# ScalarE evaluates silu of the gate in both routed runs and in ten of the sixteen shared products of a macaron layer

## The chip, the core and the metric

The kernel runs on one core of a Trainium2 chip. The metric is device time in microseconds (us); lower is better. The core's engines are called by their short names: PE (TensorE, matmuls and transposes), ACT (ScalarE), DVE (VectorE), POOL (GpSimd) and SP (SyncE, which only issues DMAs here). Each works through its own instructions in order; semaphores tie them together.

## The reference

The layer is `x + ffn/2`, then `x + ssm`, then `x + ffn/2`, each behind a layernorm, on 4 x 512 tokens of width 256. The feed-forward part stands twice and is what the change touches:

```
logits = x @ router_w                       # 8 experts, top 1
score = sigmoid(max(logits))
xs = x * score
for e in range(8):                          # each token goes to its one expert
    h = silu(xe @ gate_w[e]) * (xe @ up_w[e])
    out = out + where(token of e, h @ down_w[e], 0)
shared = silu(x @ shared_gate_w) * (x @ shared_up_w) @ shared_down_w
return out + shared
```

The part between the two is a state-space scan over 512 time steps with 16 states for each of 256 channels, in four sequences.

## The kernel before

Five semaphored programs, one for each engine, are written out by hand, so the order in the source is the order on each engine. All data is float32. There are two feed-forward runs, `r = 0` (to about 110 us of the trace) and `r = 1` (from about 331 us), and the scan stage stands between them.

**Shared products.** For each run, each of four sequences `b` and each half `fo` of the hidden width, PE computes gate and up into two PSUM banks (L865, `shared_gate_up`), ACT writes `tanh(gate/2)` to `sh_th` (L565, `shared_tanh`), and DVE makes `sh_q = (tanh+1)*gate` (L1181) and then `sh_q*up` (L1184), both in `shared_hidden`. That is 2*silu(gate)*up. PE multiplies it by the shared down weights (L845, `shared_down`), and DVE adds a quarter of the result to `x_sb` (L1286, `shared_result`); the quarter undoes the factor of 2 and applies the half of the layer. The products of `(1, 0)` are made in four smaller pieces within the scan stage (`tanh_piece`, `hidden_piece`).

**Routed runs.** Tokens are gathered by expert into 18 tiles `j` of 128 rows, even ones of one expert (whole), odd ones of four experts with 32 rows each (mixed). For a tile, PE does `gate_up(j)` (L904 for whole, L901 for mixed tiles), then `turn(j)`, which transposes the product of tile `j-1` (L914) and the gathered rows of tile `j+1` (L919), then `down(j-2)` (L941, L938). ACT does `tanh(j)` (L580), with the token's half score as its scale, then `copy(j)` of the transposed block out of PSUM (L585), then copies of expert weights (L593). DVE does `q = (tanh+1)*gate` (L1309), `h = q*up` (L1314), the scaling of the result of tile `j-2` (L1324 in run 0, L1327 in run 1), and copies of expert weights (L1296). POOL gathers rows and scatters results by indirect DMA. `gate_up(j+1)` needs `copy(j)`, and `turn(j+1)` needs `h(j)`.

**Around them.** Behind run 0, `combine` adds the scattered results, `stats_of` and `normalise` make the second layernorm, `ln_transposes` (L793) turns it, and `project` (L969) begins the scan's inputs. Ahead of run 1, `route` and `row_ids` on DVE make the list of tokens, between the shared products. ACT evaluates functions by tables; where one is needed that is not there, the program has an ACT_TABLE_LOAD.

Of the kernel before, what the change touches and what calls it, by code (L numbers as in the profile page):

```python
# [15 lines left out]
ALU = mybir.AluOpType  # L16
ACT = mybir.ActivationFunctionType
# [10 lines left out]
def macaron_kernel(nc, x, w_xT, w_dtT, b_dt, a_log, d_skip, router_w, gate_w, up_w, down_w,  # L28
# [5 lines left out]
    KC = D // P  # L34
# [41 lines left out]
    with ExitStack() as ctx:  # L76
# [3 lines left out]
        def sem(name):  # L80
# [132 lines left out]
        ff_gu, ff_tanh, ff_mul, ff_hidden, ff_tp, ff_tpc, ff_y, ff_yc = (  # L213
            sem(f"ff_{s}") for s in ("gu", "tanh", "mul", "hidden", "tp", "tpc", "y", "yc"))
# [33 lines left out]
        def shared_banks(r, b, fo):  # L248

            return (H[0], H[1]) if fo == 0 else (YS[0], YS[1]) if r == 1 or b in (0, 3) else (T, Y)  # L250

# [297 lines left out]
        def _(act):  # L549
# [10 lines left out]
            def shared_tanh(r, b, fo):  # L560
                u = 2 * BATCH * r + 2 * b + fo
                act.wait_ge(sh_gu, u + 1)
                if u >= 2:
                    act.wait_ge(sh_mul, u - 1)
                nc.scalar.activation(sh_th[:, u % 2], shared_banks(r, b, fo)[0], ACT.Tanh, scale=0.5).then_inc(sh_tanh, 1)  # L565
# [9 lines left out]
            def routed(r):  # L575
                def tanh(j):
                    act.wait_ge(ff_gu, NR * r + j + 1)
                    if r > 0 or j >= 2:
                        act.wait_ge(ff_mul, NR * r + j - 1)
                    nc.scalar.activation(th[:, j % 2], H[j % 2][:, 0:F], ACT.Tanh, scale=xr[:, j % XR, D:D + 1]).then_inc(ff_tanh, 1)  # L580

                def copy(j, lo=0, hi=4):

                    act.wait_ge(ff_tp, (NR + 2) * r + j + 2)
                    nc.scalar.activation(tt[:, (j + 1) % 2, lo:hi], T[:, lo * P:hi * P].rearrange("p (a t) -> p a t", t=P),  # L585
                                         ACT.Copy).then_inc(ff_tpc, 1)

                def part_dn(i, g):

                    e = act.value_load(part_expert(i, g), min_val=0, max_val=E - 1)  # L590
                    if i >= 2:
                        act.wait_ge(ff_y, NR * r + 2 * i - 2)
                    nc.scalar.activation(dn_part(i, g), w_dn[:, :, bass.ds(e, 1), :].squeeze(2), ACT.Copy).then_inc(wc_dn, 1)  # L593

                act.wait_ge(rt_expert, r + 1)
                if r == 0:
                    act.wait_ge(experts_in, 16 * 3 * KC)
                copy(-1, lo=2)
                for j in range(NR):
                    tanh(j)  # L600
                    copy(j, lo=2 if j == 0 else 0, hi=2 if j == NR - 1 else 4)
                    for g in ((1, 2) if j % 2 == 0 else (3,)):
                        part_dn(j // 2, g)
                copy(NR, hi=2)
# [119 lines left out]
            shared_tanh(0, 0, 0)  # L724
            route_copy(0)
            route(0)
            shared_tanh(0, 0, 1)
            for fo in range(KC):
                shared_tanh(0, 1, fo)
            routed(0)  # L730
            act.wait_ge(a_log_in, 16)
            nc.scalar.activation(a_exp[:], a_in[:], ACT.Exp).then_inc(a_ready, 1)
            act.wait_ge(a_ready, 1)
            nc.scalar.activation(a_neg[:], a_exp[:], ACT.Copy, scale=-1.0).then_inc(a_ready, 1)
            for fo in range(KC):
                shared_tanh(0, 2, fo)
            shared_tanh(0, 3, 0)
# [6 lines left out]
            shared_tanh(0, 3, 1)  # L744
# [10 lines left out]
            for fo in range(KC):  # L755
                shared_tanh(1, 1, fo)
            ln_copies(2, BATCH - 1)
            route_copy(1)
            route(1)
            for b in range(2, BATCH):  # L760
                for fo in range(KC):
                    shared_tanh(1, b, fo)
# [389 lines left out]
        def _(dve):  # L1152
# [23 lines left out]
            def shared_hidden(r, b, fo):  # L1176
# [3 lines left out]
                gate, up = shared_banks(r, b, fo)  # L1180
                nc.vector.scalar_tensor_tensor(out=sh_q[:, fo], in0=sh_th[:, fo], scalar=1.0, in1=gate,  # L1181
                                               op0=ALU.add, op1=ALU.mult).then_inc(sh_mul, 1)
                dve.wait_ge(sh_mul, u + 1)
                nc.vector.tensor_tensor(hidden_rows(r, b)[:, fo], sh_q[:, fo], up, ALU.mult).then_inc(sh_hidden, 1)  # L1184

            def hidden_piece(p):
# [5 lines left out]
                dve.wait_ge((half_mul, sh_mul)[h], n)  # L1192
# [3 lines left out]
            def route(r):  # L1196
# [14 lines left out]
                nc.vector.tensor_scalar(xn_no[:, :, D], score[:, 2], 0.5, None, ALU.mult)  # L1211
                nc.vector.scalar_tensor_tensor(out=xn_no[:, :, D + 1], in0=score[:, 2], scalar=0.25, in1=score[:, 2],
                                               op0=ALU.mult, op1=ALU.mult).then_inc(rt_score, 1)
# [91 lines left out]
            def routed(r):  # L1305
                def hidden(j):
                    u = j % 2
                    dve.wait_ge(ff_tanh, NR * r + j + 1)
                    nc.vector.scalar_tensor_tensor(out=q_sb[:, u], in0=th[:, u], scalar=1.0, in1=H[u][:, 0:F],  # L1309
                                                   op0=ALU.add, op1=ALU.mult).then_inc(ff_mul, 1)  # L1310
                    dve.wait_ge(ff_mul, NR * r + j + 1)
                    if j >= 2:
                        dve.wait_ge(ff_tp, (NR + 2) * r + j + 1)
                    nc.vector.tensor_tensor(h_sb[:, u], q_sb[:, u], H[u][:, F:], ALU.mult).then_inc(ff_hidden, 1)  # L1314
# [222 lines left out]
```

## Time and profile before

| | us |
|---|---|
| median of three runs | 443.85 |
| fastest and slowest of them | 442.93, 444.07 |
| span of the profiled execution | 441.9 |
| PE busy | 403.1 (91%) |
| DVE busy | 349.3 (79%) |
| POOL busy | 280.9 (64%) |
| ACT busy | 271.2 (61%) |

No own time is listed for the profiled execution apart from its span, from its first to its last instruction. The median lies 1.95 us above that span. A row of a timeline gives the start, the duration, the engine, the line, the operation, what it writes and reads, how many instructions are merged in it, and in brackets the idle time of the engine before it with what ended that.

### The profile page before, as it was taken

The page shows a single profiled execution, that of the slowest core. Times are in us where ns is not written, and L with a number is a line of the kernel's source. Part 1 is how long each engine was busy: PE and PEld are TensorE (multiplying, and loading weights), DVE is VectorE, ACT ScalarE, POOL GpSimd, SP SyncE. Part 2 cuts the span into 40 slices and gives each one's busy share as a digit, 9 for nine tenths or more (in the row PEclk, how much of TensorE's full clock was granted, in tenths as well). Part 3 has the DMA queues.
Part 4 walks back from the last instruction along what each step waited for, and adds up shares of the span by engine and source line. Part 5 has one row for each costly group of instructions (what it writes and reads, how often), then busy time and mean ns, then how long its engine had stood idle before and what let it go on. Part 6 is the DMA issues. An engine that isn't in the chain of part 4 may idle for free. (4 is left out here: it accounts for less than half of the span.)

```text
span 441.9 us, 8372 instructions
## 1 busy us (share of the span) xinstructions
PE 403.1 (91%) x2716; PEld 278.5 (63%) x2716; DVE 349.3 (79%) x564; ACT 271.2 (61%) x498; POOL 280.9 (64%) x216
## 2 busy tenths in 40 slices
PE   6899899999896899899989998989999898899995
PEld 6437444444354689777977797879984556344442
DVE  5689666674598988999999999989886876567762
ACT  1410555564148799897999899997952110556552
POOL 7204356543337589997999799989881006577543
PEclk9899999999999999999999999999999999999998
DMA  8968115942604227463537353452320634234411
GB/s 257 384 181 251 48 59 174 296 163 85 202 34 66 73 79 177 85 143 108 182 75 132 133 168 74 119 158 94 122 58 0 196 91 117 92 117 135 120 52 44
DMA packets 50808, 56.84 MB, mean 129 GB/s; under 512 B 16329, under 2 KB 35597, under 8 KB 50768
## 3 DMA queue, kind: packets, MB, share of 16 engines
q1 hardware_dynamic: 46624, 45.78, 35.5%
q0 software_dynamic: 4144, 10.54, 8.0%
q8 instruction: 23, 0.38, 0.3%
q14 instruction: 17, 0.14, 0.1%
HBM read 41.14 MB, written 16.48 MB: 130 GB/s over the span
## 5 line engine op out<-in xcount | busy, mean ns | idle before, releaser
L515 POOL TENSOR_TENSOR gs<-hs,c_sb 128x1024 f32<-128x1024 f32 x63 | 148.3, 2377 | 19.2 <-DVE hs L1407 12.0
L1407 DVE TENSOR_TENSOR_SCAN hs<-da,bank 128x1024 f32<-128x1024 f32 x64 | 144.1, 2273 | 4.1 <-PE bank L1016 2.1
L652 ACT ACTIVATE da<-dt_sb,a_neg 128x511 f32<-128x511 f32 x128 | 84.4, 711 | 2.4 <-DVE dt_sb L1370 1.2
L1040 PE MATMUL bank<-ident,gs 128*128 128x128 f32 x504 | 66.3, 275 | 7.3 <-POOL gs L515 5.7
L1040 PEld LDWEIGHTS bank<-ident,gs 128*128 128x128 f32 x504 | 56.0, 141 | 12.0 <-POOL gs L515 9.6
L668 ACT ACTIVATE dbx_t<-dtx_t,h_sb 128x256 f32<-128x256 f32 x145 | 62.0, 496 | 1.6 <-DVE dtx_t L1376 1.4
L865 PE MATMUL bank<-xnT,w_gu 128*128 128x512 f32 x112 | 51.2, 605 | 0.0
L1016 PE MATMUL bank<-ident,dbx_t 128*128 128x128 f32 x336 | 44.2, 274 | 6.7 <-DVE hs L1407 3.8
L469 POOL DMA_INDIRECT da<-rows,row_token x29 | 30.3, 1046 | 30.5 <-issue 30.1
L1016 PEld LDWEIGHTS bank<-ident,dbx_t 128*128 128x128 f32 x336 | 37.6, 141 | 12.0 <-DVE hs L1407 5.8
L580 ACT ACTIVATE th<-bank,da 128x256 f32<-128x256 f32 x36 | 17.1, 474 | 43.4 <-PE bank L904 30.7
L565 ACT ACTIVATE hs<-bank 128x512 f32<-128x512 f32 x14 | 8.4, 597 | 54.3 <-PE bank L865 48.9
L904 PE MATMUL bank<-w_gu,tt 128*128 x72 | 35.6, 616 | 3.2 <-ACT tt L585 2.2
L469 POOL DMA_INDIRECT da<-rows,row_half x14 | 15.0, 1073 | 36.2 <-DVE row_token L1280 27.1
L490 POOL DMA_INDIRECT token_out<-y_sb,row_token x18 | 19.0, 1054 | 29.4 <-DVE y_sb L1324 26.9
L901 PE MATMUL bank<-w_gu,tt 128*32 x72 | 34.3, 598 | 1.4 <-ACT tt L585 1.4
L1309 DVE SCALAR_TENSOR_TENSOR q_sb<-th,bank 128x256 f32<-128x256 f32 x36 | 15.1, 420 | 25.7 <-ACT th L580 25.7
L865 PEld LDWEIGHTS bank<-xnT,w_gu 128*128 128x128 f32 x112 | 21.1, 195 | 22.6 <-issue 22.5
L901 PE MATMUL bank<-dtx_t,tt 128*32 128x512 f32 x72 | 34.3, 598 | 0.0
L585 ACT ACTIVATE tt<-bank 128x512 f32<-128x512 f32 (+1 forms) x40 | 22.1, 554 | 15.2 <-PE bank L919 13.5
L490 POOL DMA_INDIRECT out<-y_sb,row_token x18 | 19.5, 1084 | 17.0 <-DVE y_sb L1327 9.6
L554 ACT ACTIVATE xnT<-bank 128x512 f32<-128x512 f32 x24 | 13.8, 589 | 18.9 <-PE bank L793 18.9
(179 smaller groups left out, 802.0 us busy)
## 6 DMA issues: line engine op xcount, KB each, us to landing
c_sb<-c_dram SPq DMA_DIRECT2D x64, 256.0 KB, 3.3
rows<-xn_no SPq DMA_DIRECT2D x8, 516.0 KB, 5.7
diag_dram<-dbx_t SPq DMA_DIRECT2D x6, 512.0 KB
routing<-diag_dram SPq DMA_DIRECT2D x11, 256.0 KB, 2.8
slot_m<-diag_dram SPq DMA_DIRECT2D x11, 256.0 KB, 2.8
rows<-xn_no SPq DMA_DIRECT2D x1, 2064.0 KB, 9.5
x_sb<-in_x SPq DMA_DIRECT2D x4, 512.0 KB, 5.8
w_gu<-in_gate_w SPq DMA_DIRECT2D x2, 1024.0 KB, 10.0
```

The source lines that it names most:

```text
L469: nc.gpsimd.indirect_dma_start(out=xr[:, u, lo:hi], out_offset=None, in_=source, in_offset=bass.IndirectOffsetOnAxis(ap=row, axis=0), boun ...
L490: nc.gpsimd.indirect_dma_start(out=rows_back, out_offset=bass.IndirectOffsetOnAxis(ap=row_token[:, TILE[j]:TILE[j] + 1], axis=0), in_=y_sb ...
L515: nc.gpsimd.tensor_tensor(gs[:, s % 2], hs[:, s % RING], c_sb[:, s % RING].unsqueeze(1).to_broadcast([P, KC, L]), ALU.mult).then_inc(sc_g, 1)
L585: nc.scalar.activation(tt[:, (j + 1) % 2, lo:hi], T[:, lo * P:hi * P].rearrange("p (a t) -> p a t", t=P), ACT.Copy).then_inc(ff_tpc, 1)
L652: nc.scalar.activation(da[:, s % RING, k, 1:L], dt_sb[:, k, seq(s // N)][:, 1:L], ACT.Exp, scale=a_neg[:, k, s % N:s % N + 1]).then_inc(sc ...
L668: step = nc.scalar.activation(plain_buffer(s)[:, i, :], dtx_t[:, b % 2, i, :], ACT.Copy, scale=b_t[:, b, i, n:n + 1])
L865: last = nc.tensor.matmul(shared_banks(r, b, fo)[h], w_gu[:, k, SHARED, h * F + fo * P:h * F + (fo + 1) * P], xnT[:, k, b * L:(b + 1) * L] ...
L901: last = nc.tensor.matmul(H[j % 2][part, :], tt[:, j % 2, 2 + k, part], gu_part(i, g)[:, k, :] if g else w, start=(k == 0), stop=(k == KC ...
L904: last = nc.tensor.matmul(H[j % 2][:, :], tt[:, j % 2, 2 + k], w, start=(k == 0), stop=(k == KC - 1))
L1016: mm = nc.tensor.transpose(DBX[s % 2][:, k, i * P:(i + 1) * P], plain_buffer(s)[:, i, k * P:(k + 1) * P], ident[:])
L1040: mm = nc.tensor.matmul(YA[k][:, i * P:(i + 1) * P], products[:, k, i * P:(i + 1) * P], ident[:], start=(s % N == 0 and i == 0), stop=(s % ...
L1407: nc.vector.tensor_tensor_scan(hs[:, s % RING].rearrange(flat), da[:, s % RING].rearrange(flat), DBX[s % 2][:, :, :].rearrange(flat), 0.0, ...
```

## The change

In both routed runs ACT evaluates `silu(score*gate)`, and DVE multiplies it by `up`. In run 0's shared products `(0,0,1)`, `(0,1,*)`, `(0,2,*)`, `(0,3,0)` and run 1's `(1,2,*)`, `(1,3,*)`, ten in all by the function `by_silu`, ACT evaluates `silu(gate)`, and DVE multiplies it by 2 and by `up` in one instruction. The other six keep tanh. The row scales kept beside each token become the score and half the score. The exponential of `a_log`, and its wait for that input, move from behind run 0 to its front, and ACT gets three explicit table loads (`preload_act_table`). ACT waits for the whole product two back (`sh_hidden`, `ff_hidden`), where it waited for the first of its two DVE instructions (`sh_mul`, `ff_mul`).

```
+        def by_silu(r, b, fo):
+            return (r, b, fo) not in ((0, 0, 0), (0, 3, 1)) and (r, b) not in ((1, 0), (1, 1))
+        def by_tanh(u):
+            return sum(not by_silu(t // (2 * BATCH), t // 2 % BATCH, t % 2) for t in range(u + 1))
...
-            def shared_tanh(r, b, fo):
+            def shared_gate(r, b, fo):
                 u = 2 * BATCH * r + 2 * b + fo
                 act.wait_ge(sh_gu, u + 1)
                 if u >= 2:
-                    act.wait_ge(sh_mul, u - 1)
-                nc.scalar.activation(sh_th[:, u % 2], shared_banks(r, b, fo)[0], ACT.Tanh, scale=0.5).then_inc(sh_tanh, 1)
+                    act.wait_ge(sh_hidden, u - 1)
+                if by_silu(r, b, fo):
+                    nc.scalar.activation(sh_th[:, u % 2], shared_banks(r, b, fo)[0], ACT.Silu).then_inc(sh_tanh, 1)
+                else:
+                    nc.scalar.activation(sh_th[:, u % 2], shared_banks(r, b, fo)[0], ACT.Tanh, scale=0.5).then_inc(sh_tanh, 1)
...
-                def tanh(j):
+                def gate(j):
                     act.wait_ge(ff_gu, NR * r + j + 1)
                     if r > 0 or j >= 2:
-                        act.wait_ge(ff_mul, NR * r + j - 1)
-                    nc.scalar.activation(th[:, j % 2], H[j % 2][:, 0:F], ACT.Tanh, scale=xr[:, j % XR, D:D + 1]).then_inc(ff_tanh, 1)
+                        act.wait_ge(ff_hidden, NR * r + j - 1)
+                    nc.scalar.activation(th[:, j % 2], H[j % 2][:, 0:F], ACT.Silu, scale=xr[:, j % XR, D:D + 1]).then_inc(ff_gate, 1)
...
-            shared_tanh(0, 0, 0)
+            shared_gate(0, 0, 0)
             route_copy(0)
             route(0)
-            shared_tanh(0, 0, 1)
-            for fo in range(KC):
-                shared_tanh(0, 1, fo)
-            routed(0)
             act.wait_ge(a_log_in, 16)
             nc.scalar.activation(a_exp[:], a_in[:], ACT.Exp).then_inc(a_ready, 1)
+            nc.scalar.preload_act_table(ACT.Silu)
             act.wait_ge(a_ready, 1)
             nc.scalar.activation(a_neg[:], a_exp[:], ACT.Copy, scale=-1.0).then_inc(a_ready, 1)
+            shared_gate(0, 0, 1)
             for fo in range(KC):
-                shared_tanh(0, 2, fo)
-            shared_tanh(0, 3, 0)
+                shared_gate(0, 1, fo)
+            routed(0)
+            for fo in range(KC):
+                shared_gate(0, 2, fo)
+            shared_gate(0, 3, 0)
+            nc.scalar.preload_act_table(ACT.Exp)
             ln_copies(1, 0)
...
             route(1)
+            nc.scalar.preload_act_table(ACT.Silu)
...
             def shared_hidden(r, b, fo):
...
+                if by_silu(r, b, fo):
+                    nc.vector.scalar_tensor_tensor(out=hidden_rows(r, b)[:, fo], in0=sh_th[:, fo], scalar=2.0, in1=up,
+                                                   op0=ALU.mult, op1=ALU.mult).then_inc(sh_hidden, 1)
+                    return
...
-                nc.vector.tensor_scalar(xn_no[:, :, D], score[:, 2], 0.5, None, ALU.mult)
-                nc.vector.scalar_tensor_tensor(out=xn_no[:, :, D + 1], in0=score[:, 2], scalar=0.25, in1=score[:, 2],
-                                               op0=ALU.mult, op1=ALU.mult).then_inc(rt_score, 1)
+                nc.vector.tensor_copy(xn_no[:, :, D], score[:, 2])
+                nc.vector.tensor_scalar(xn_no[:, :, D + 1], score[:, 2], 0.5, None, ALU.mult).then_inc(rt_score, 1)
...
-                    dve.wait_ge(ff_tanh, NR * r + j + 1)
-                    nc.vector.scalar_tensor_tensor(out=q_sb[:, u], in0=th[:, u], scalar=1.0, in1=H[u][:, 0:F],
-                                                   op0=ALU.add, op1=ALU.mult).then_inc(ff_mul, 1)
-                    dve.wait_ge(ff_mul, NR * r + j + 1)
+                    dve.wait_ge(ff_gate, NR * r + j + 1)
                     if j >= 2:
                         dve.wait_ge(ff_tp, (NR + 2) * r + j + 1)
-                    nc.vector.tensor_tensor(h_sb[:, u], q_sb[:, u], H[u][:, F:], ALU.mult).then_inc(ff_hidden, 1)
+                    nc.vector.tensor_tensor(h_sb[:, u], th[:, u], H[u][:, F:], ALU.mult).then_inc(ff_hidden, 1)
```

## Rows read from the trace of the kernel before

**Rows 1.** Busy time of each engine in scan stage and run 1's loop (x instructions).

```profile
145.00:331.00 186.00, 173.91 (x1380) 155.63 (x1378) 175.96 (x157) 166.66 (x314) 169.67 (x86) 1.00 0.44 118
...
377.00:432.00 55.00, 53.52 (x381) 24.67 (x384) 37.55 (x73) 33.78 (x60) 34.74 (x32) 1.00 0.33 97
```

**Rows 2.** Timeline, a step of run 1's loop; last row: the chain that ended last.

```profile
390.20 0.60 ACT L585 ACTIVATE tt<-bank 128x512 f32<-128x512 f32 x1
...
390.73 0.42 DVE L1314 TENSOR_TENSOR h_sb<-q_sb,bank 128x256 f32<-128x256 f32 x1
...
390.96 0.62 PE L901 MATMUL bank<-w_gu,tt 128*32 x1
...
392.88 0.37 PE bank L914 x2
```

**Rows 3.** Groups by line and shape: busy us, mean ns, idle before.

```profile
L565 ACT ACTIVATE hs<-bank 128x512 f32<-128x512 f32 x14 | 8.4, 597 | 54.3 <-PE bank L865 48.9 <-DVE hs L1181 5.4
L626 ACT ACTIVATE dt_sb<-bank,b_sb 128x512 f32<-128x512 f32 x8 | 5.5, 681 | 0.0
L646 ACT ACT_TABLE_LOAD x4 | 5.1, 1283 | 0.1
L1181 DVE SCALAR_TENSOR_TENSOR hs<-hs,bank 128x512 f32<-128x512 f32 x14 | 9.5, 676 | 8.5 <-ACT hs L565 8.5
```

**Rows 4.** Timeline of PE and DVE at the ends of both routed runs.

```profile
106.17 0.41 PE L914 MATMUL bank<-ident,h_sb 128*128 128x128 f32 x2 [0.23 <-DVE h_sb L1314]
...
433.47 0.42 DVE L1309 SCALAR_TENSOR_TENSOR q_sb<-th,bank 128x256 f32<-128x256 f32 x1 [1.91 <-ACT th L580]
...
433.93 0.42 DVE L1314 TENSOR_TENSOR h_sb<-q_sb,bank 128x256 f32<-128x256 f32 x1
...
434.50 0.41 PE L914 MATMUL bank<-ident,h_sb 128*128 128x128 f32 x2 [0.23 <-DVE h_sb L1314]
...
435.38 1.12 PE L941 MATMUL bank<-w_dn,tt 128*128 x4 [0.47 <-ACT tt L585]
```

**Rows 5.** Timeline of DVE and PE between run 0 and the scan.

```profile
119.92 0.65 DVE L1181 SCALAR_TENSOR_TENSOR hs<-hs,bank 128x512 f32<-128x512 f32 x1
...
121.35 1.99 PE L845 MATMUL bank<-w_dn,gs 128*128 128x256 f32 x8 [1.67 <-DVE gs L1184]
...
121.52 1.38 DVE L1173 TENSOR_SCALAR xn_no<-x_sb,mv,rstd 128x256 f32<-128x256 f32 x4 [0.23 <-POOL rstd L447]
...
123.18 1.04 PE L793 MATMUL bank<-ident,xn_no 128*128 128x128 f32 x8
...
125.78 1.88 PE L969 MATMUL bank<-xnT,w_x 128*96 128x512 f32 x4
```

**Rows 6.** Timeline of PE and DVE ahead of run 1's loop.

```profile
366.05 3.62 PE L845 MATMUL bank<-w_dn,gs 128*128 128x256 f32 x16
...
366.91 0.67 DVE L1181 SCALAR_TENSOR_TENSOR hs<-hs,bank 128x512 f32<-128x512 f32 x1
...
370.37 3.69 PE L845 MATMUL bank<-w_dn,gs 128*128 128x256 f32 x16 [0.71 <-DVE x_sb L1286]
```

**Rows 7.** Timeline of PE ahead of run 0's loop.

```profile
35.91 2.25 PE L770 MATMUL bank<-ident 128*128 128x128 f32 x18
38.28 5.54 PE L845 MATMUL bank<-w_dn,gs 128*128 128x256 f32 x24
```

**Rows 8.** ACT's and SP's timeline where the change puts work; last, a DMA's landing time.

```profile
19.84 0.43 SPq L324 DMA_DIRECT2D a_in<-in_A_log  x1
...
28.15 0.60 ACT L565 ACTIVATE hs<-bank 128x512 f32<-128x512 f32 x1 [3.20 <-PE bank L865]
...
123.82 1.08 ACT L554 ACTIVATE xnT<-bank 128x512 f32<-128x512 f32 x2 [3.50 <-PE bank L793]
...
350.99 0.60 ACT L565 ACTIVATE hs<-bank 128x512 f32<-128x512 f32 x1 [6.64 <-PE bank L865]
...
a_in<-in_A_log SPq DMA_DIRECT2D x1, 16.0 KB, 4.9
```

More of the change, by code:

```diff
@@ L212, in macaron_kernel @@
             sem(f"sh_{s}") for s in ("gu", "tanh", "mul", "hidden", "y", "x"))
-        ff_gu, ff_tanh, ff_mul, ff_hidden, ff_tp, ff_tpc, ff_y, ff_yc = (
-            sem(f"ff_{s}") for s in ("gu", "tanh", "mul", "hidden", "tp", "tpc", "y", "yc"))
+        ff_gu, ff_gate, ff_hidden, ff_tp, ff_tpc, ff_y, ff_yc = (
+            sem(f"ff_{s}") for s in ("gu", "gate", "hidden", "tp", "tpc", "y", "yc"))
         ff_in = [sem(f"ff_in{u}") for u in range(XR)]
@@ L599, in routed @@
                 for j in range(NR):
-                    tanh(j)
+                    gate(j)
                     copy(j, lo=2 if j == 0 else 0, hi=2 if j == NR - 1 else 4)
@@ L743, in _ @@
             project_ln(0)
-            shared_tanh(0, 3, 1)
+            shared_gate(0, 3, 1)
             act.wait_ge(a_ready, 2)
@@ L755, in _ @@
             for fo in range(KC):
-                shared_tanh(1, 1, fo)
+                shared_gate(1, 1, fo)
             ln_copies(2, BATCH - 1)
@@ L759, in _ @@
             route(1)
+            nc.scalar.preload_act_table(ACT.Silu)
             for b in range(2, BATCH):
                 for fo in range(KC):
-                    shared_tanh(1, b, fo)
+                    shared_gate(1, b, fo)
             routed(1)
@@ L1180, in shared_hidden @@
                 gate, up = shared_banks(r, b, fo)
+                if by_silu(r, b, fo):
+                    nc.vector.scalar_tensor_tensor(out=hidden_rows(r, b)[:, fo], in0=sh_th[:, fo], scalar=2.0, in1=up,
+                                                   op0=ALU.mult, op1=ALU.mult).then_inc(sh_hidden, 1)
+                    return
                 nc.vector.scalar_tensor_tensor(out=sh_q[:, fo], in0=sh_th[:, fo], scalar=1.0, in1=gate,
                                                op0=ALU.add, op1=ALU.mult).then_inc(sh_mul, 1)
-                dve.wait_ge(sh_mul, u + 1)
+                dve.wait_ge(sh_mul, by_tanh(u))
                 nc.vector.tensor_tensor(hidden_rows(r, b)[:, fo], sh_q[:, fo], up, ALU.mult).then_inc(sh_hidden, 1)
@@ L1191, in hidden_piece @@
                                                op0=ALU.add, op1=ALU.mult).then_inc((half_mul, sh_mul)[h], 1)
-                dve.wait_ge((half_mul, sh_mul)[h], n)
+                dve.wait_ge((half_mul, sh_mul)[h], by_tanh(n - 1) if h else n)
                 nc.vector.tensor_tensor(hidden_rows(1, 0)[:, fo, part], th[:, 1], T[:, L // 2:],
```

## The prediction

> **What bounds the kernel now.** I read the busy time of each engine by stage first, because an average over the whole span mixes two kinds of stage. In the loop of run 1, PE is busy for 53.52 of 55 us and DVE for 37.55; in the scan stage DVE is busy for 175.96 of 186 us [rows 1]. The change takes DVE work out of the routed loops, where PE is the limit, and leaves the scan stage, where DVE is the limit, alone. So the work removed is not the gain: I looked for the places where PE waits for one of the removed instructions.
>
> Then the timeline of one step of the loop. The product h is done at 390.73 + 0.42 = 391.15, and PE turns it at 392.88, 1.73 us later [rows 2]. In the steady loop nobody waits for DVE. ACT's copy is another matter: it ends at 390.80, the next gate-up starts at 390.96 [rows 2], and a released PE instruction starts about 0.15 us after its releaser (434.50 against the end of h at 434.35 [rows 4]). So the copy, which stands behind the activation in ACT's queue, has almost no slack.
>
> Last, the chain that ended last and PE's idle brackets, outside the loops. PE waits for a removed DVE instruction at the end of both runs (0.23 us each [rows 4]), between run 0 and the scan (1.67 us [rows 5]), and ahead of run 1 (0.71 us [rows 6]).
>
> **The change, part by part.**
>
> *Removed on DVE.* Ten shared products lose one instruction of 0.68 us [rows 3], in effect 0.70 with the gap behind it; 36 routed products lose one of 0.42, in effect 0.46, the distance of the two starts in [rows 4]. That is 10 x 0.70 + 36 x 0.46 = 23.6 us of DVE time. In the loops it is hidden behind PE, at a gain of nothing. It counts at five places:
>
> 1. *Ahead of run 0's loop.* Three products in a row end 2.1 us earlier on DVE, but PE is warming until 35.91 + 2.25 = 38.16, and starts the down product at 38.28 [rows 7]. The warming is late next: 0.1 us.
>
> 2. *End of run 0.* PE waits 0.23 us for the last h [rows 4], which now comes 0.46 earlier. PE itself is free 0.23 earlier, and that bounds the transposes. The next product, L941, starts 0.88 us behind their start; the profile blames ACT's copy, but by the code this product does not need that last copy, so I take the 0.47 us of idle time as PE's own issue latency, which runs from the moment the wait is met. Then all of 0.46 passes on. Bounds: 0.23 if the copy does release it, 0.70 (0.23 + 0.47) if the gap goes altogether. I take 0.46. The scatter, the DMA back and `combine` follow in one chain.
>
> 3. *Between run 0 and the scan.* Product (0,2,1) starts at 119.92 and now ends 0.70 earlier, so PE starts its down product at 120.65 instead of 121.35 [rows 5]. PE then does that (1.83 us, to the 123.18 of the transposes), eight transposes, half a down product and `project`, at 125.78 [rows 5]. The transposes need the normalised rows: 121.52 + 1.38 = 122.90 for the last, and those do not move, since they wait for POOL's rstd. From 120.65 PE reaches the transposes at 122.48; the first half takes some 0.5 us and covers the wait for the last row. So `project` starts about 0.67 earlier. If the transposes had to wait for all four rows, it would be 123.18 - 122.95 = 0.23. I take 0.67, as the first four transposes need only the first two rows. Behind `project` the chain is PE, ACT, DVE in turns, each waiting for the other, up to the first scan step, which PE, ACT and DVE then keep filled.
>
> 4. *Ahead of run 1's loop.* Products (1,3,0) and (1,3,1) follow each other on DVE from 366.91 [rows 6], with the addition behind them for which PE waits. They end 1.4 us earlier, but PE is at the down product of (1,2) until 366.05 + 3.62 = 369.67. So PE gains its whole wait, 370.37 - 369.67 = 0.70 [rows 6], and is then the limit. I take 0.68. Product (1,2,0), earlier in this stage, also shortens, hidden behind PE's gate-up.
>
> 5. *End of run 1.* As at the end of run 0, 0.46 (0.23 to 0.70), straight to the last scatter.
>
> *Silu for tanh on ACT.* The trace has no silu. The nearest rows are tanh of 128x512 at 597 ns, and the dearest other function on that shape, 681 [rows 3]. The lower bound is no difference: these rows give no reason for a gain. The upper bound is 0.084 us for each tile whose copy has no slack, so 36 x 0.084 = 3.0 us if no tile has any. I take nothing, since the shapes, sources and scales stay, and tanh is the nearest row.
>
> *Table loads.* Three more, each 1.28 us [rows 3]. They stand where ACT is idle: 3.20 us ahead of 28.15, 3.50 ahead of 123.82, 6.64 ahead of 350.99 [rows 8]. Cost nothing; without that cover 3 x 1.28 = 3.8 us, if each lay on the chain.
>
> *Moved.* The wait for `a_log`, its exponential and its copy now stand ahead of (0,0,1). Queued behind them are that silu, for which DVE waits, and all later ACT work. The load is issued at 19.84 and lands 4.9 us later, at 24.7, and ACT is idle from 28.15 - 3.20 = 24.95 on [rows 8]. Of the 3.20 us one table load takes 1.28, and 1.9 are left for two activations of 128x32, smaller than the 128x512 one of 0.60. It costs nothing; if it ran late by a microsecond, DVE would still be at its list of tokens, and the product would be late only behind that. No DMA is moved past another.
>
> *Waits on whole products and the score columns.* A product two back has long ended in every case but (0,1,1), where the now single instruction ends when the first of the two did. The two score instructions become two others on 128x16. Nothing.
>
> *Sum.* 0.10 + 0.46 + 0.67 + 0.68 + 0.46 = 2.37 us. The span of 441.9 becomes 439.5; with the 1.95 us that lie between span and median, 443.85 becomes 441.5.
>
> **The rivals.** A measurement of this kernel tells a change of 0.3% from none, that is 1.3 us: faster means below 442.5, slower above 445.2.
>
> *The activation's table lacks copy.* The routed loop alternates the gate activation with copies on ACT. If silu's table had no copy, each step would need loads of 1.28 us, and the one ahead of L585 would fall on the copy's missing slack: 36 x 1.25 = 45 us, some 487 us. It decides as soon as one load per step stands between gate and copy. For it: the trace has no silu, and a function's absence does show as pairs of loads around Ln [rows 3]. Against it: copies run beside exp and tanh without loads. The Trainium skill, page "ScalarE: Activation LUTs", section "Table sets: the hidden batching unit", speaks for loads by named sets, and says that cheap functions such as copy fill every set; by that this rival does not occur. No row here shows silu's set.
>
> *Part of the gain stays behind.* If `project` gains only 0.23, and each end 0.23, the sum is 0.10 + 0.23 + 0.23 + 0.68 + 0.23 = 1.47, so 442.4. A silu dearer by a quarter of its bound (0.75 us) on top makes it 443.1. For it: each of these chains has a second condition close behind. Against it: each was followed to its next wait above. The same page, section "What happens when an `exp` ACTIVATE runs", says that the rate per element is the same for every function; by that the dearer silu falls away, and the sum is 442.4.
>
> *Nothing arrives.* The scan stage, 186 us with its own waits on PE, POOL and transfers, may swallow what comes before it (1.23 us), and the chain ahead of run 1 may be held by the gather: 0.46 is left, 443.4. Against it: DVE, busy 95% of that stage [rows 1], starts earlier and has no less time.
>
> [...]
>
> **How the numbers follow.** The forecast, 441.5, gets 0.50, with a range of its own from 440.8 to 442.4. More gets 0.12, part 0.20, nothing 0.10, and the table rival 0.08. The range from 440.2 to 443.3 takes in the forecast, more and part, with half a microsecond for fetches below, and leaves out nothing and the table rival, 0.18. Faster: 0.50 + 0.12 + half of part 0.10 = 0.72. Same: 0.10 + 0.10 = 0.20. Slower: 0.08.
>
> **What the profile after would show.** Two DVE instructions become one in ten shared and 36 routed products. A step of the routed loop keeps its length (a wait of PE in it would show the table rival, or a dear silu, at once). The idle times of 0.23 ahead of the last L914 go, L941 starts within about 0.25 to 0.3 us of PE being free, the 1.67 ahead of L845 falls to about 1.0, and the 0.71 ahead of the last shared down product goes to nothing. ACT_TABLE_LOADs rise by three and none of them stands within a loop. The prediction is wrong if a load appears beside L585, if silu is longer than tanh by 0.05 us or more, or if the first scan step does not start some 1.2 us earlier.

## The result, and the profile after

The changed kernel takes 441.87 us in the median of 20 executions (440.35 to 443.35), the kernel before 444.34 us (442.67 to 447.92) in as many: the ratio is 0.9944, with a 95% interval of 0.9923 to 0.9957. That is 0.6% faster; the forecast was 441.5. The profiled execution's span went from 441.9 to 439.6 us.

Within one kernel the time of an execution goes with its mean granted clock, so I compared equal clocks too. At 0.999 to 1.000 the changed kernel took 440.35 to 440.67 us (four executions), the kernel before 442.73 to 443.21 (nine, timed beside the experiments below). The middles of the two are 2.4 us apart, as the medians are.

First the busy times of the stages of [rows 1], for the same lengths of time (columns: the stretch, its length, then PE, PE's weight loads, DVE, ACT and POOL, the granted clock, the DMA share, GB/s).

```profile
144.20:330.20 186.00, 173.69 (x1381) 155.56 (x1379) 176.00 (x157) 166.63 (x314) 169.56 (x86) 1.00 0.43 118
375.20:430.20 55.00, 53.52 (x382) 24.66 (x384) 31.22 (x56) 33.54 (x60) 34.82 (x32) 1.00 0.33 100
```

In 55 us of run 1's loop DVE fell from 37.55 to 31.22 us, and PE is busy for the same 53.52 us. Over the whole span DVE fell from 349.3 to 329.5 us, PE from 403.1 to 402.4. So 20 us of DVE went away for 2.3 us of span.

The groups by line and shape (busy us, mean ns, idle time before) that answer to [rows 3]:

```profile
L591 ACT ACTIVATE th<-bank,da 128x256 f32<-128x256 f32 x36 | 17.0, 473 | 43.1 <-PE bank L918 30.4 <-PE bank L915 12.7
L596 ACT ACTIVATE tt<-bank 128x512 f32<-128x512 f32 x32 | 19.1, 597 | 1.3
L574 ACT ACTIVATE hs<-bank 128x512 f32<-128x512 f32 x10 | 6.0, 597 | 40.0 <-PE bank L879 34.6 <-DVE gs L1196 5.4
L576 ACT ACTIVATE hs<-bank 128x512 f32<-128x512 f32 x4 | 2.4, 597 | 11.6 <-PE bank L879 11.6
```

Silu (L574) takes 597 ns and tanh (L576) 597 on the same tile; the gate's silu (L591) takes 473, where its tanh took 474. The copy (L596) still takes 597 ns. No load of a table stands between the two in the loop, so silu's table has copy. The Trainium skill ("ScalarE: Activation LUTs", "Table sets: the hidden batching unit") says that cheap functions, copy among them, are in every set; the trace agrees.

The three added loads, in ACT's timeline (start, length, engine, line):

```profile
25.54 1.28 ACT L740 ACT_TABLE_LOAD   x1
...
120.15 1.28 ACT L750 ACT_TABLE_LOAD   x1
...
343.52 1.28 ACT L773 ACT_TABLE_LOAD   x1
```

All three lie in idle time of ACT, none in a loop. The ends of the runs, in the timeline of PE and DVE, answer to [rows 4]:

```profile
106.06 0.44 PE L928 MATMUL bank<-ident,h_sb 128*128 128x128 f32 x2
106.88 1.13 PE L955 MATMUL bank<-w_dn,tt 128*128 x4 [0.38 <-DVE y_sb L1338]
...
431.69 0.42 DVE L1328 TENSOR_TENSOR h_sb<-th,bank 128x256 f32<-128x256 f32 x1 [1.90 <-ACT th L591]
...
432.41 0.44 PE L928 MATMUL bank<-ident,h_sb 128*128 128x128 f32 x2
433.13 1.13 PE L955 MATMUL bank<-w_dn,tt 128*128 x4 [0.28 <-DVE y_sb L1341]
```

The transposes (L928, L914 before) no longer wait; the down product (L955, L941 before) starts 0.72 to 0.82 us behind them instead of 0.88 to 0.89. The handover from run 0 to the scan answers to [rows 5]:

```profile
119.74 0.65 DVE L1196 SCALAR_TENSOR_TENSOR gs<-hs,bank 128x512 f32<-128x512 f32 x1
...
120.45 1.99 PE L859 MATMUL bank<-w_dn,gs 128*128 128x256 f32 x8 [0.95 <-DVE gs L1196]
...
121.34 1.38 DVE L1187 TENSOR_SCALAR xn_no<-x_sb,mv,rstd 128x256 f32<-128x256 f32 x4 [0.95 <-POOL rstd L455]
122.28 1.16 PE L807 MATMUL bank<-ident,xn_no 128*128 128x128 f32 x8
...
125.00 1.88 PE L983 MATMUL bank<-xnT,w_x 128*96 128x512 f32 x4
```

PE's wait went from 1.67 to 0.95 us. The transposes L807 start 0.94 us behind the first normalised row's start, with the other rows still to come: they take 1.16 us instead of 1.04 and hide that wait. Ahead of run 1's loop [rows 6] and of run 0's [rows 7] PE's timeline now reads:

```profile
36.35 2.25 PE L784 MATMUL bank<-ident 128*128 128x128 f32 x18
38.44 5.52 PE L859 MATMUL bank<-w_dn,gs 128*128 128x256 f32 x24
...
365.21 7.07 PE L859 MATMUL bank<-w_dn,gs 128*128 128x256 f32 x32
```

The 32 products ahead of run 1 stand in one row: the wait of 0.71 us between them is gone.

**Where the time came from.** I cut both profiled executions at the same instructions, and give each segment in us from start to start, so that a modelled end of a matmul does not count. "Warming" are PE's products ahead of run 0 whose result nobody reads (L784, L770 before):

| segment | before | after | gained |
|---|---|---|---|
| warming of PE to run 0's first gate product | 9.69 | 9.40 | 0.29 |
| run 0's loop, to its last gate product | 58.37 | 58.39 | -0.02 |
| end of run 0, to the last two down products | 3.09 | 2.74 | 0.35 |
| scatter and DMA, to `combine` | 9.86 | 9.87 | -0.01 |
| `combine` to `project` (the handover) | 8.86 | 8.25 | 0.61 |
| `project` to the first scan step | 17.79 | 17.78 | 0.01 |
| scan stage and what follows, to the down product of (1,1) | 208.16 | 208.11 | 0.05 |
| from there to run 1's first transposes (the entry to run 1) | 22.17 | 21.22 | 0.95 |
| transposes to first gate product | 1.00 | 1.01 | -0.01 |
| run 1's loop and its end | 60.48 | 60.01 | 0.47 |
| to the last scatter | 3.72 | 3.74 | -0.02 |

The sum is 2.67 us. The profiled execution after began 0.44 us later with its warming (36.35 against 35.91). That distance is there already at the first layernorm's transposes (17.37 against 16.93), ahead of every instruction that the change touches: 2.67 - 0.44 = 2.23, and the spans, given to 0.1 us, differ by 2.3.

### The profile page after: what moved, and what is told of

Read it like the earlier page. It is cut to its first block and busy times, and to the rows that moved or that the text cites. A ratio compares the mean times of both kernels' runs of the same rounds, so it can differ in the third digit from the quotient of the medians.

```text
span 439.6 us, 8329 instructions
## 1 busy us (share of the span) xinstructions
PE 402.4 (92%) x2716; PEld 278.4 (63%) x2716; DVE 329.5 (75%) x518; ACT 275.0 (63%) x501; POOL 281.1 (64%) x216
## 5 line engine op out<-in xcount | busy, mean ns | idle before, releaser
L591 ACT ACTIVATE th<-bank,da 128x256 f32<-128x256 f32 x36 | 17.0, 473 | 43.1 <-PE bank L918 30.4
L1328 DVE TENSOR_TENSOR h_sb<-th,bank 128x256 f32<-128x256 f32 x36 | 15.1, 420 | 28.0 <-ACT th L591 27.9
L574 ACT ACTIVATE hs<-bank 128x512 f32<-128x512 f32 x10 | 6.0, 597 | 40.0 <-PE bank L879 34.6
L596 ACT ACTIVATE tt<-bank 128x512 f32<-128x512 f32 (+1 forms) x40 | 22.1, 553 | 13.6 <-PE bank L933 12.3
```

## The experiments

Every ratio is against the kernel before, timed on the same chip beside the experiment.

**One half each.** In the first kernel only the routed products use silu, in the second only the shared ones; the tables are loaded at the borders.

```
 # routed only: shared products stay tanh and two DVE instructions
-            return (r, b, fo) not in ((0, 0, 0), (0, 3, 1)) and (r, b) not in ((1, 0), (1, 1))
+            return False
 # shared only: routed products stay tanh and two DVE instructions
-  ACT.Silu, scale=xr[:, j % XR, D:D + 1]).then_inc(ff_gate, 1)
+  ACT.Tanh, scale=xr[:, j % XR, D:D + 1]).then_inc(ff_gate, 1)
```

> Only the 36 routed products use silu; all sixteen shared products keep tanh and two VectorE instructions; the table loads stand in ScalarE's idle time around the routed runs. My theory (the gain comes only from the places where TensorE waited for a removed instruction): only the two ends of the routed runs are left, some 0.4 us each, so 0.8 us faster than the kernel before, and the span from the first scan step to the last is unchanged. Rival (VectorE relief in the loops helps by itself, in proportion to the work removed): 36 x 0.46 of 23.6 us, 70% of the 2.4 us gain, 1.7 us faster.

> Only the ten shared products use silu; the routed runs keep tanh and two VectorE instructions, with five explicit table loads, each in idle time of ScalarE. My theory: the three places around the loops are left, 0.3 ahead of run 0, 0.6 ahead of the scan and 0.9 ahead of run 1, so 1.8 us faster than before, and TensorE waits 0.23 us for h at the ends of both runs again. Rival (in proportion to VectorE work removed): 30% of 2.4, 0.7 us faster. If the two extra table loads were not hidden, 1.3 us of the gain would go for each.

Shared only: 442.57 us, 0.9948 (0.9928 to 0.9969). By the medians that is -1.8, as the theory said, by the ratio -2.3. The waits at both ends are those of before, to the hundredth:

```profile
106.19 0.41 PE L931 MATMUL bank<-ident,h_sb 128*128 128x128 f32 x2 [0.23 <-DVE h_sb L1335]
107.07 1.12 PE L958 MATMUL bank<-w_dn,tt 128*128 x4 [0.47 <-ACT tt L596]
```

Routed only missed: 445.25 us, 1.0012 (0.9990 to 1.0035), no gain. The two ends gained what they should (3.09 to 2.72, 60.48 to 60.02). But `combine` to `project` took 10.53 us instead of 8.86. PE's timeline there, then busy times and granted clock (the third column from the end) of two stretches:

```profile
121.63 2.65 PE L859 MATMUL bank<-w_dn,gs 128*128 128x256 f32 x8 [2.02 <-DVE gs L1202]
124.07 1.91 PE L807 MATMUL bank<-ident,xn_no 128*128 128x128 f32 x8
```

```profile
122.00:124.00 2.00, 2.00 (x8) 1.59 (x7) 2.00 (x5) 0.00 (x0) 0.00 (x0) 0.70 0.03 8
124.00:126.00 2.00, 2.00 (x10) 1.93 (x9) 1.93 (x8) 0.60 (x1) 0.00 (x0) 0.50 0.00 0
```

The wait ahead of the shared down product is 2.02 us here, against 1.67 before and 0.95 in the changed kernel. Behind it the granted clock fell to 0.50, the level of 1.2 GHz: the products took 2.65 us instead of 1.99 and the transposes 1.91 instead of 1.04. In the kernels before and after the clock stayed at 1.00 there. The time agrees: in eleven of this kernel's twelve executions the mean granted clock was 0.983 to 0.991. So I tried the same kernel with seven products in that wait whose result nobody reads (two records each in the trace):

```
+            warm(YA[1], 7)
             shared_down(0, 2, (0,))
```

> The kernel with only the routed products in silu, and seven warming transposes of the identity ahead of the first half of shared down product (0,2), where TensorE waited 2.02 us in that kernel and the granted clock fell to 0.5 of full behind it. My theory: the fallen clock there cost the 1.7 us that the stretch from combine to project took longer than in the kernel before (10.53 against 8.86), and hid a gain of 0.8 us; with the clock held that stretch takes 8.9 us again and the kernel is 0.8 us faster than before (0.998). Rival (something else in the routed-only kernel costs it, a table load or the order of ScalarE): still as slow as before, and the stretch stays above 10 us.

```profile
119.93 1.72 PE L784 MATMUL bank<-ident 128*128 128x128 f32 x14
122.12 1.99 PE L859 MATMUL bank<-w_dn,gs 128*128 128x256 f32 x8 [0.47 <-DVE gs L1203]
```

```profile
122.00:124.00 2.00, 1.88 (x9) 1.62 (x10) 1.77 (x6) 0.00 (x0) 0.19 (x1) 1.00 0.00 0
124.00:126.00 2.00, 2.00 (x15) 1.87 (x14) 1.97 (x5) 1.09 (x2) 0.00 (x0) 1.00 0.00 0
```

The clock stays at 1.00 and the segment takes 8.86 us again: the fall of the clock behind the wait was the cost. In the median this kernel takes 444.21 us, 0.9992 (0.9969 to 1.0015), 1.0 us less than without the products, but hardly less than before: -0.33 and -0.52 at the ends are eaten by +0.37 up to `combine` and +0.34 ahead of run 1. The latter stands between DVE's three copies of expert weights: the third starts 1.86 us behind the first, 1.54 before, with a second pause marked issue of 0.24 us. So the gain of 0.8 that I had expected of the routed half is seen at its two ends, but in no median.

**DVE work back in the loops.** 32 DVE instructions of 128x256 on otherwise unused memory, one in each step of the loops but the last two:

```
                     hidden(j)
+                    if j < NR - 2:
+                        pad(F)
```

> The changed kernel, with one more VectorE instruction of 128x256 (about 0.42 us) behind each of the first 16 products of either routed run, on operands that nothing else waits for: 32 x 0.42 = 13.4 us of VectorE work back, but none of it ahead of h. My theory: the same time as the changed kernel, 2.3 us faster than before. Rival (VectorE's relief in the loops counts): about 1.4 us of the gain goes, 1.0 us faster than before.

441.66 us, 0.9927 (0.9904 to 0.9949): the gain is whole, and the two loops take 58.41 us and, with the end, 60.01, as in the changed kernel. DVE's relief in the loops is worth nothing.

**DVE work back at the five places only.** An instruction of the removed one's size ahead of the shared products (0,2,1), (1,3,0), (1,3,1) and of the last routed product of each run; the rest of the change stays.

```
+                    if (r, b, fo) in ((0, 2, 1), (1, 3, 0), (1, 3, 1)):
+                        pad(2 * F)
...
+                    if j == NR - 1:
+                        pad(F)
```

> The changed kernel, with five VectorE instructions put back at the places where TensorE waited: one of 128x256 ahead of the last product of each routed run, one of 128x512 ahead of the shared products (0,2,1), (1,3,0) and (1,3,1); 41 of the 46 removed instructions stay away. My theory: 0.36 + 0.47 + 0.61 + 0.95 = 2.4 us come back, so nothing is left but some 0.2 us ahead of run 0: the time of the kernel before within 0.3%. Rival (gain in proportion to work removed): these five put back 2.9 of 23.6 us, 0.3 us, so still 2.0 us faster than before.

443.55 us, 0.9992 (0.9964 to 1.0021): five instructions give most of the gain back. All of it is not shown: the median still lies 0.8 us below the kernel before, and of the 2.4 us that I had put on these places the segments give back 1.3. The end of run 0 took 2.97, run 1 60.35, the handover 8.74 us, but the entry to run 1 only 21.48, a quarter of the 0.95. Besides, the scan segment took 0.7 us more in the profiled execution, where the granted clock fell to 0.55, 0.50 and 0.50 from 140 to 146 us. PE had been busy for 1.05 and 1.09 of 2 us in the two stretches ahead. One execution of the changed kernel (below) shows that fall too, so it is no effect of the pads. At a mean granted clock of 0.995 to 0.996, the highest it had, this kernel took 443.02 to 443.57 us; the changed kernel took 440.94 to 442.49 there, the kernel before beside it 443.29 to 444.50.

**No explicit loads of tables.** The three preloads are left out, so a load comes where the first activation needs it.

```
-            nc.scalar.preload_act_table(ACT.Silu)
...
-            nc.scalar.preload_act_table(ACT.Exp)
...
-            nc.scalar.preload_act_table(ACT.Silu)
```

> The changed kernel without its three explicit table loads, so that each load stands directly ahead of the first activation that needs it, behind that one's waits. My theory: the load for the exponential then lies on ScalarE's chain from project to the first scan step, 1.28 us; the one ahead of (0,0,1) and the one ahead of (1,2,0) only eat idle time of VectorE. So 1.3 us slower than the changed kernel, 1.1 us faster than before. Rival (table loads are hidden wherever they stand): the changed kernel's time, 2.4 us faster than before.

442.53 us, 0.9956 (0.9934 to 0.9978). ACT's timeline:

```profile
27.08 1.28 ACT L574 ACT_TABLE_LOAD   x1
...
133.34 1.28 ACT L641 ACT_TABLE_LOAD   x1
134.64 1.06 ACT L641 ACTIVATE w_exp<-w_exp 128x1024 f32<-128x1024 f32 x1
```

The load of exp now stands between activations that follow one another, and `project` to the first scan step takes 19.26 us instead of 17.78: 1.48 on the path. The medians show 0.7 of it (442.53 against 441.87); why not all is open. The load of silu at 27.08 was harmless: it directly follows the activation ahead (26.83 + 0.23), before PE has the tile that silu waits for. The next activation starts 1.30 us behind the load's start. The Trainium skill ("ScalarE: Activation LUTs", "What ACT_TABLE_LOAD costs") gives 1283 ns and a drain of about 1380 besides for each switch; the trace agrees on the first and shows no drain behind this one.

**ACT's slack in the loop.** One more copy of 128x128 on ACT in each step, between gate activation and copy.

```
                     gate(j)
+                    nc.scalar.activation(q_sb[:, 1, 0:P], w_gu[:, 0, SHARED, 0:P], ACT.Copy)
```

> The changed kernel, with one more ScalarE copy of 128x128 (SBUF to SBUF, some 0.2 us of its time) between the gate activation and the copy of each of the 36 tiles. My theory (ScalarE's copy has next to no slack in the step of a whole tile, some 0.1 to 0.2 in that of a mixed one): 18 x 0.2 = 3.6 us slower than the changed kernel or more, so 1.2 us slower than before: that much a silu dearer than tanh by 0.2 us would have cost. Rival (the loop is bound by TensorE alone, with slack for ScalarE): the changed kernel's time.

442.86 us, 0.9956 (0.9935 to 0.9978), 1.0 above the changed kernel; in the profiled execution the loops take 0.66 and 1.03 more (59.05 and 61.04 us). I had expected 3.6. ACT's timeline in one step:

```profile
391.87 0.47 ACT L591 ACTIVATE th<-bank,da 128x256 f32<-128x256 f32 x1 [0.87 <-PE bank L916]
392.25 0.30 ACT L612 ACTIVATE q_sb<-w_gu 128x128 f32<-128x128 f32 x1
392.44 0.59 ACT L596 ACTIVATE tt<-bank 128x512 f32<-128x512 f32 x1
```

The copy starts 0.57 us behind the activation. Without the extra instruction it started 0.56 behind it in this kind of step (391.16 and 391.72) and 0.43 in the other kind (387.98 and 388.41). So the extra copy delays nothing in half of the steps, and 0.14 us in the others: 18 x 0.14 = 2.5 us at most, and a part of that is slack.

**The pause ahead of the last two down products.** By my theory it is PE's load of the expert's number into a register. I expected the first of the two edits below to take 0.7 us off the changed kernel's time, the second 1.0. First both loads just ahead of the last transposes, then, in another kernel, ahead of the last gate product, where PE has work queued:

```
 # just ahead of the last transposes
+                e_last = [down_expert(j) for j in (NR - 2, NR - 1)]
                 turn(NR)
 # or, in the loop, ahead of the last gate product
+                    if j == NR - 1:
+                        e_last = [down_expert(n) for n in (NR - 2, NR - 1)]
                     gate_up(j)
```

> The changed kernel, with TensorE's two register loads of the expert numbers for the last two down products taken ahead of its wait for the last h of each routed run. My theory (the pause of 0.3 to 0.5 us between the last transposes and L955 is TensorE's own register load behind the wait, not a wait for ScalarE's copy or VectorE's result): L955 follows the transposes at once, 0.4 us earlier at the end of run 0 and 0.3 at the end of run 1: 0.7 us faster than the changed kernel, 3.1 us faster than before. Rival (the releaser that the profile names holds it): the changed kernel's time.

> The changed kernel with the two register loads of each run's last two down products (the expert's number) taken by TensorE before its last gate product, where TensorE has work queued and nothing to wait for. Theory: the pause of 0.25 to 0.68 us at each run's end is TensorE's own register load, issued behind the wait; taken before the last step it costs nothing there, the first down product starts about 0.25 us after the transposes and these are not late. End of run 0 from 2.74 to about 2.2 us, end of run 1 from 60.01 to about 59.5 us (loop and end together), in total about 1.0 us less than the changed kernel's time. Rival: the load stops TensorE wherever it is issued, about half a us each, and only moves into the loop: then nothing is gained.

The first took 441.95 us, 0.9930 (0.9906 to 0.9955), the second 441.59 us, 0.9941 (0.9916 to 0.9965). PE's timeline, of the first at the end of run 0:

```profile
105.69 0.41 PE L928 MATMUL bank<-ident,h_sb 128*128 128x128 f32 x2 [0.68 <-issue]
105.94 1.11 PE L960 MATMUL bank<-w_dn,tt 128*128 x4
```

and of the second at the end of run 0, in run 1's last step, and at its end:

```profile
106.31 0.44 PE L928 MATMUL bank<-ident,h_sb 128*128 128x128 f32 x2
106.59 1.03 PE L960 MATMUL bank<-w_dn,tt 128*128 x4
...
429.80 0.61 PE L915 MATMUL bank<-w_gu,tt 128*32 x1 [0.83 <-issue]
...
433.03 0.44 PE L928 MATMUL bank<-ident,h_sb 128*128 128x128 f32 x2
433.30 1.03 PE L960 MATMUL bank<-w_dn,tt 128*128 x4
```

With the load out of the way the down product follows the transposes after 0.25 to 0.28 us. So the pause is the register load, and not ACT's last copy, which ran at 106.79 in the second kernel, behind the start of the product it was blamed for. The trace has the load itself, among the instructions of PE's sequencer (marked q, not counted as busy). In the changed kernel, at the end of run 0 and over the whole span (the three numbers are the least, the median and the greatest duration in ns, then the first and last start):

```profile
L939 PEldq TENSOR_LOAD <-expert x1: 372/372/372, 106.0 to 106.0; - x1
...
L939 PEldq TENSOR_LOAD <-expert x36: 296/302/1005, 52.1 to 433.3; - x36
```

The load starts behind the met wait, its last register instruction at 106.6, and the down product at 106.88.

But the load stops PE elsewhere: ahead of the transposes in the first kernel (0.68), inside the last step in the second (0.16 us in run 0, whose loop took 58.58 us against 58.39; 0.83 in run 1). Of those 0.83 us a good part is chance: two of the three loads that stand there took 0.552 and 0.523 us, where the same program took 0.298 to 0.308 in the next kernel, with a pause of 0.16. In the second kernel the end of run 0 went to 2.19 us as the theory said, and run 1 took 60.46, worse than 60.01; in the first they took 2.91 and 60.12, both worse than in the changed kernel (2.74 and 60.01). Neither is faster than the changed kernel by more than the intervals tell.

**With products in PE's waits, and the changed kernel again.** The second kernel above with nine products that nobody reads:

```
+            warm(YA[1], 3)
             shared_down(0, 2, (0,))
...
+            warm(H[0], 6)
             turn_dbx(0)
```

> The kernel above with nine TensorE products more whose result nobody reads: three ahead of the shared down product between run 0 and the scan, six ahead of the transposes that enter run 1. They fill stretches in which TensorE stands idle. Theory: these stretches are waits that the products do not lengthen, and the granted clock was 0.99 to 1.00 in most executions, so at most 0.3 to 0.6 us less in the median than the kernel above. Rival: the products are late themselves and push the shared down product or the transposes: 0.2 to 0.5 us more.

> The changed kernel itself, timed beside the two above: 441.9 us, 0.6% under the kernel before.

The six stand ahead of the first scan step's transposes (138.03 us), not ahead of run 1 as my expectation has it. 442.16 us, 0.9955 (0.9934 to 0.9976): nothing gained, nothing lost. Its profiled execution had the shortest span, 438.9 (the first kernel above had 438.9 too), with run 1 at 59.74 us, but the median does not follow. The changed kernel again: 441.76 us, 0.9953 (0.9937 to 0.9969). In its profiled execution the ends take 2.75 and 60.01, the handover 8.26 and the entry to run 1 21.23 us: these four terms repeat. The first does not, by PE's timeline:

```profile
36.06 2.25 PE L784 MATMUL bank<-ident 128*128 128x128 f32 x18
38.15 3.62 PE L859 MATMUL bank<-w_dn,gs 128*128 128x256 f32 x16
42.17 1.99 PE L859 MATMUL bank<-w_dn,gs 128*128 128x256 f32 x8 [0.40 <-DMA w_dn<-in_down_w]
```

The down product starts 2.09 us behind the warming's start, as in the execution above (2.37 before). Then PE waits 0.40 us for the load of weights, and the segment takes 9.89, more than before. That is the rule and not the exception: in the ten profiled executions of the changed kernel and of the variants that keep silu in its shared products, this segment took 9.40 to 10.00 us, 9.79 in the middle, and seven of them show the wait, of 0.27 to 0.52 us. The 0.29 of the first table is luck.

## Why the prediction was right

The time came out 0.4 us above the forecast, and by the mechanism forecast: DVE's relief in the loops is worth nothing (the kernel with 32 instructions put back loses nothing), and what it is worth at a few places where PE waits is the gain (five instructions put back there take most of it away). The terms, us:

| step of the prediction | forecast | measured |
|---|---|---|
| 1, ahead of run 0's loop | 0.10 | 0.29 in the first execution, -0.20 in the second; -0.10 in the middle of ten |
| 2, end of run 0 | 0.46 | 0.35 |
| 3, between run 0 and the scan | 0.67 | 0.61 |
| 4, ahead of run 1's loop | 0.68 | 0.95 |
| 5, end of run 1 | 0.46 | 0.47 |
| sum | 2.37 | 2.67 in the profiled execution; the medians differ by 2.47 |

That the sum fits so well is luck in part. Step 4 gave 0.27 us more than forecast, steps 2 and 3 gave 0.17 less, and step 1 gave nothing over several executions, 0.10 less. Steps 2 to 5 alone make 2.38.

*Step 1* named the warming as what is late next, and took its end from the row's length. That end is modelled: the next product starts 2.09 us behind the warming's start, with a length of 2.25 given. Behind that I did not look for a second wait, and there is one, the load of `w_dn`. So this term was mis-sized: 0.10 forecast, and nothing gained in most executions.

*Steps 2 and 5* rested on the reading that the idle time blamed on ACT's copy is PE's own, and runs from the moment that the wait is met. In run 1 the down product starts 1.03 us behind the end of h before (434.35 and 435.38), 1.02 after (432.11 and 433.13); the kernels with early register loads show what it is. In run 0 the distance grew from 1.03 to 1.13, which is the missing 0.1; 0.06 of it is the register load, 0.311 us before and 0.372 after. The forecast that L955 would follow within 0.25 to 0.3 us of PE being free holds for run 1 (0.28), not for run 0 (0.38).

*Step 3* chose 0.67, against 0.23 if the transposes had waited for all four rows. They did not; I put the 0.12 us that they take longer down to the last row. (The 122.95 in the second sum does not follow from the rows, which give 122.90 for the last row; the 0.67 does not rest on it.)

*Step 4* was mis-sized: 0.95 for 0.68. The bracket of 0.71 is idle time behind a modelled end. In the run of 32 products without a wait 16 take 6.90 / 2 = 3.45 us, while the row of before gives 3.62 for them; before, the second 16 started 370.37 - 366.05 = 4.32 us behind the first. 4.32 - 3.45 = 0.87, and 0.08 more stand behind the last product (3.53 to the transposes instead of 3.45). What made DVE late is not the two removed instructions alone. Ahead of the copies of expert weights DVE paused 0.89 us, marked issue, in the kernel before; it pauses 0.41 in both profiled executions of the changed one. The trace has what stands there: DVE's register load of the expert's number for the first copy. Before, then after:

```profile
364.78 1.61 DVE L1296 COPY c_sb<-w_gu 128x1024 f32 x2 [0.89 <-issue]
...
L1293 DVEq TENSOR_LOAD <-expert x1: 787/787/787, 363.6 to 363.6; - x1
...
363.46 1.44 DVE L1313 COPY c_sb<-w_gu 128x1024 f32 x2 [0.41 <-issue]
...
L1310 DVEq TENSOR_LOAD <-expert x1: 305/305/305, 362.7 to 362.7; - x1
```

The load took 0.48 us less, and so did the pause. The prediction had no term for it. The five pads, with a load of 0.302 and a pause of 0.40, brought back only 0.26. In the shared-only kernel the load took 0.305, but the pause was 0.77, the rest of it behind the load; with the shared products on silu the entry still takes 21.22 us. So the change covers the long pause and also comes without it; either would do for most of the 0.95. Why the load took 0.30 us in ten of the thirteen profiled executions, and 0.77 to 0.79 in the three of kernels whose shared products keep two instructions, is open.

*What was put at nothing:* silu for tanh, the loads of tables, the moved wait for `a_log` (its exponential ran at 25.30) and the score columns show no cost in these segments, as forecast. The step of the loop keeps its length. One sentence was too strong: that the copy has almost no slack. Its slack is 0.13 us in half of the steps, and an ACT instruction more per step cost 1.0 to 1.7 us, not 3.6.

*The rivals.* No load came beside the copy, so the table rival falls. "Nothing arrives" falls with the scan segment, which took 208.11 us for 208.16 and swallowed nothing. "Part stays behind" (442.4) lies 0.5 us from the result, and "more", with PE's pause of 0.47 gone at both ends (441.0), 0.9; the segments speak for neither, since steps 3 and 5 came nearly whole and the pause stayed. The half microsecond for instruction fetches in the range is shown by no run; the pauses marked issue that I followed at these places were register loads, or stood behind one.

The prediction's own sign, a first scan step some 1.2 us earlier, did not show: it starts 0.79 us earlier, 0.29 + 0.35 + 0.61 = 1.25 less the later start of 0.44. It was a poor sign, because an absolute time takes in how early the execution came to the change: the warming began between 35.01 and 36.35 us in eight profiled executions whose program up to there is the same.

*What I had not seen* is a rival that the routed half alone would have met: a longer wait of PE in the handover, with the fall of its clock. The full change shortens that wait by the shared product, and so does not come near it.

## What to carry to other kernels

Where one engine fills a loop, work taken from another is worth nothing there: walk PE's waits outside the loops one by one, take what each can give, and ask what is late next. Measure from start to start across a wait, not by the idle bracket behind a modelled end. A change that lengthens a wait of PE by a third of a microsecond can cost more than that when the granted clock falls behind it, so try the halves of a change before you trust that their sum is made of them. A pause marked issue can hide a register load: ask the trace for the line that takes the register.

## What the runs showed of the hardware

- Behind a wait of 2.02 us PE's granted clock fell to 0.50 (1.2 GHz) for the stretch that followed; behind 1.67 us at the same place it stayed at 1.00 (2.4 GHz). What PE did ahead of the wait was much the same. The length of the idle time alone does not tell: from 138 to 140 us PE was busy for 0.56 of 2 us in the execution where the clock then fell, and for 0.29 to 0.67 in four executions where it stayed at 1.00. One execution of the changed kernel also ran at 0.50 from 140 to 146 us, in the first scan steps, behind stretches where PE was busy for 0.95 and 0.56 of 2 us.
- A register load on PE showed as a pause wherever it stood, in the last step of a run too, where PE had work queued (0.16 to 0.20 us in three of four last steps, 0.83 in the fourth). Its own duration varies: 0.30 us in the median of 36, up to 1.0; on DVE 0.31 in the median of 54, up to 1.1 (changed kernel). What makes one long is open.
- The time of an execution went with its mean granted clock: the kernel before took 442.73 to 442.98 us at 1.000 and 445.61 to 447.66 at 0.983 on one chip. Medians of ten to twelve executions that differ by less than 1 us can differ by that alone.
- An automatic load of a table is placed right behind the previous activation, ahead of the wait of the one that needs it (27.08 us), so that it can be hidden without being asked for.
